# Softmax row sums in the attention of two layers: kept by ScalarE's exponentials and spread by one identity product, in place of products with ones

## The chip, the cores and the metric

The kernel runs on one core of one Trainium2 chip. The metric is the device time of the whole launch in microseconds. The engines are TensorE (PE, with its weight loads shown as PEld), VectorE (DVE), ScalarE (ACT), GpSimd (POOL) and SyncE (SP), whose DMA queue is SPq.

## The reference

Four layers, each an attention or a lookup ("xattn") and a feed-forward part, every one added to x through a gate. Layers 1 and 3 have the attention that the change touches; layer 1 has rotated queries and keys and a causal mask, layer 3 a given mask:

```python
# x: [32, 128, 128] (batch, position, width); H = 16 heads of width 8
q = split_heads(layernorm(x) @ Wq.T + bq)
k = split_heads(ctx @ Wk.T + bk)
v = split_heads(ctx @ Wv.T + bv)
# layer 1: q, k = rope(q), rope(k)
scores = jnp.einsum('bhqd,bhkd->bhqk', q, k) / sqrt(8)
scores = where(mask, scores, -inf)
probs = softmax(scores, axis=-1)
out = einsum('bhqk,bhkd->bhqd', probs, v).reshape(B, S, 128)
x = x + tanh(g_xattn[layer]) * (out @ Wo.T + bo)
```

## The kernel before

`build` runs nine stages one after the other, with a barrier between them; `stage_attn` (L949) is called for layer 1 (names `L1_...`) and for layer 3 (`L3_...`). The trace leaves the layer's number out, so both are `L_...`.

**Tiling.** The 32 batches are taken in 8 groups of 4 (`NG`, `GB`). The 16 heads of a batch are taken in 4 head groups of 4 heads (`NHG`). A step k is one batch and one head group: `hg = k % 4`, batch `b = k // 4`, 16 steps (`UG`) to a group of batches, 128 steps to a layer. All engines walk the same steps, each in its own order written out by hand, and wait for each other through counting semaphores.

**A step.** TensorE's `scores(k)` (L1328) makes a 128x512 tile of scores in one of two PSUM banks `sc`: 128 queries by 4 heads of 128 keys, and adds the mask by a second product. VectorE's `maximum(k)` (L1169) takes the negated row maxima of each head into `negm`. ScalarE's `exponent(k)` (L1255) does four exponentials of 128x128, one for each head, from `sc` into `E`. TensorE's `turn(k)` (L1337) transposes them into a bank `pt`, and ScalarE's `move(k)` (L1265) copies that to `PT`. TensorE's `attend(k)` (L1346) then adds to the bank `pp` of the batch: columns 0 to 127 get the products with the values `VZ`, columns 128 to 255 the products with ones `OZ`. Each is four products with 32 weight columns. The values and the ones stand at the places of their heads in otherwise zero tiles, so after four steps `pp` has all 16 heads, 8 rows each, and under 128 the row sum of the head, repeated in its 8 rows. VectorE's `invert(b)` (L1174) takes the reciprocal of the sums and `divide(b)` (L1178) multiplies.

**Order.** In TensorE's loop (L1364) step k brings `scores(k)`, `turn(k - 2)`, and in odd steps `attend(k - 5)` and `attend(k - 4)`; behind them stand, at the steps of `PUT`, the projections `put` of the next group, and at step 9 the output product `output` of the last one. `scores(k)` waits until the exponentials of step k - 2 are done, since there are two banks. ScalarE's loop (L1278) is `exponent(k)`, `move(k - 2)`, and at the steps of `UPPER` (3 and 7 in layer 1, 2 and 6 in layer 3) one more copy `upper` of keys or queries. VectorE's loop (L1211) has before `maximum(k)`: `invert` at every fourth step, `normalise` at step 0, `take` of the projections at the steps of `TAKE`, `add_output` at 11 and row statistics at 12; after it `divide` and the rest. GpSimd adds the two halves of the rotation (L1087, layer 1) and subtracts for the low parts of the split (L1089). SyncE writes the split keys and queries to memory and reads them back spread over partitions (`spread`, L1045); TensorE waits for them at the start of a group (L1365).

The attention of layer 2 (`stage_l2_attn`, L1677) has four exponentials of 128x128 with a kept sum (`accum_out`) at L1778.

Of the kernel before, what the change touches and what calls it, by code (L numbers as in the profile page):

```python
# [20 lines left out]
ACT = mybir.ActivationFunctionType  # L21
AX = mybir.AxisListType

B, S, D = 32, 128, 128
# [6 lines left out]
H, HD = 16, 8  # L31
# [913 lines left out]
NHG = 4  # L945
# [3 lines left out]
def stage_attn(nc, p, d, name, gate, rope, first):  # L949
# [4 lines left out]
    TAKE = {"k": 1, "kr": 2, "x": 3, "q": 5, "qr": 6, "v": 9}  # L954
    UPPER = {"k": 3, "q": 7} if rope else {"k": 2, "q": 6}
    OUT_PUT, OUT_TAKE = 9, 11
    TURN, ATTEND, DIVIDE = 2, 4, 8
    NU = NG * UG
    turn_of = {("const", 0): 0}
# [11 lines left out]
    with Stage(nc, name) as st:  # L971
# [8 lines left out]
        bias = {k: bias_all[:, i:i + 1] for i, k in enumerate(bn)}  # L980
        if rope:
# [8 lines left out]
        QS = [st.sb(f"QS{u}", [128, NHG, GD], F32R) for u in range(2)]  # L990
        VZ = [st.sb(f"VZ{u}", [128, GB, NHG * 128]) for u in range(2)]
        OZ = st.sb("OZ", [128, NHG * 128])
        negm = st.sb("negm", [128, 4, NHG])
        E = [st.sb(f"E{i}", [128, 512]) for i in range(4)]
        PT = [st.sb(f"PT{i}", [128, 512]) for i in range(4)]
# [6 lines left out]
        pp = [st.bank(f"pp{i}") for i in range(2)]  # L1002
        s = {k: st.sem(k) for k in (
            "w_in", "c_in0", "c_in1", "v_step", "xn_ready", "aux_full", "aux_free0", "aux_free1",
            "q_split", "k_split", "q_put", "k_put", "q_taken", "k_taken", "q_sum", "k_sum", "q_hi", "k_hi",
            "sc_ready", "max_ready", "exp_done", "pt_ready", "pt_moved", "av_done", "inv_done", "OT_ready", "v_ready", "const_ready", "zeroed", "VZ_zeroed", "QS_zeroed")}
        s_qin = [st.sem(f"q_in{u}") for u in range(2)]
        s_kin = [st.sem(f"k_in{u}") for u in range(2)]
        NW = 5 if rope else 4
# [66 lines left out]
        @block.gpsimd  # L1076
        def _(g):
            def zero(u):
                if first:
                    nc.gpsimd.memset(p.KS[u][:].bitcast(F32), 0.0).then_inc(s["zeroed"], 1)  # L1080
                else:
                    g.sem_inc(s["zeroed"], 1)

            def split(k, n):
                if rope:
                    g.wait_ge(s[k + "_taken"], n + 1)
                    nc.gpsimd.tensor_tensor(t1[k][:], t1[k][:], t2[k][:], ALU.add).then_inc(s[k + "_sum"], 1)  # L1087
                g.wait_ge(s[k + "_hi"], n + 1)
                nc.gpsimd.tensor_tensor(lo[k][:], t1[k][:], hi[k][:].bitcast(F32), ALU.subtract)\  # L1089
                    .then_inc(s[k + "_split"], 1)  # L1090

            def zero_rest(u):
                nc.gpsimd.memset(QS[u][3 * HW:128, :, :].bitcast(F32), 0.0).then_inc(s["QS_zeroed"], 1)

            zero(0)
            split("k", 0)
            split("q", 0)
            g.wait_ge(s["q_split"], 1)
            zero_rest(0)
            g.wait_ge(s["QS_zeroed"], 1)  # L1100
            zero(1)
            g.wait_ge(s["zeroed"], 2)
            zero_rest(1)
            g.wait_ge(s["QS_zeroed"], 2)
            credit(g, (tail.rstd_done, 2))
            for n in range(NG):
                if n + 1 < NG:
                    split("k", n + 1)
                if n + 1 < NG:
                    split("q", n + 1)  # L1110
                if n:
                    tail.gpsimd(g, n - 1, (n - 1) % 2)
            tail.gpsimd(g, NG - 1, (NG - 1) % 2)

        @block.vector
        def _(v):
# [52 lines left out]
            def maximum(k):  # L1169
                v.wait_ge(s["sc_ready"], k + 1)  # L1170
                nc.vector.tensor_reduce(negm[:, k % 4, :], sc[k % 2][:].rearrange("p (h k) -> p h k", h=NHG),  # L1171
                                        AX.X, ALU.max, negate=True).then_inc(s["max_ready"], 1)

            def invert(b):  # L1174
                v.wait_ge(s["av_done"], NHG * (b + 1))
                nc.vector.reciprocal(rinv[b % 2][:], pp[b % 2][:, 128:256]).then_inc(s["inv_done"], 1)

            def divide(b):  # L1178
# [32 lines left out]
            for n in range(NG):  # L1211
                for w in range(UG):
                    k = n * UG + w
                    b, due = (k - DIVIDE) // NHG, k >= DIVIDE and k % NHG == 0
                    if due:
                        invert(b)
                    if n + 1 < NG:
                        if w == 0:
                            normalise(n + 1)
                        for use in uses:  # L1220
                            if TAKE[use] == w:
                                take(use, n + 1)
                    if n:
                        if w == OUT_TAKE:
                            add_output(n - 1)
                        if w == OUT_TAKE + 1:
                            steps.need(mark)
                            mark = tail.row_stats(v, n - 1, (n - 1) % 2, steps)
                        if w == OUT_TAKE + 2:
                            steps.need(mark)  # L1230
                            tail.hand_over(v, n - 1, (n - 1) % 2)
                    maximum(k)
                    if due:
                        divide(b)
                    if n and w == OUT_TAKE:
                        mark = add_constant(n - 1)
                    if n and w == OUT_TAKE + 1:
                        steps.need(mark)
                        mark = tail.combine(v, n - 1, (n - 1) % 2, steps)
            for b in range(B - 2, B):  # L1240
                invert(b)
                divide(b)
# [5 lines left out]
        def _(a):  # L1248
# [4 lines left out]
                nc.scalar.activation(hi[k][:], t1[k][:], ACT.Copy).then_inc(s[k + "_hi"], 1)  # L1253

            def exponent(k):  # L1255
                e = E[k % 4]
                a.wait_ge(s["max_ready"], k + 1)
                if k >= 4:
                    a.wait_ge(s["pt_ready"], k - 3)
                for h in range(NHG):  # L1260
                    ins = nc.scalar.activation(e[:, h * 128:(h + 1) * 128], sc[k % 2][:, h * 128:(h + 1) * 128],  # L1261
                                               ACT.Exp, bias=negm[:, k % 4, h:h + 1])
                ins.then_inc(s["exp_done"], 1)

            def move(k):  # L1265
# [12 lines left out]
            for n in range(NG):  # L1278
                for w in range(UG):
                    k = n * UG + w  # L1280
# [10 lines left out]
        def _(t):  # L1291
# [54 lines left out]
            def attend(k):  # L1346
                n, j, hg = k // UG, k // NHG % GB, k % NHG
                if k % UG == 0:
                    t.wait_ge(s["v_ready"], n + 1)
                b = k // NHG  # L1350
                if hg == 0 and b >= 2:
                    t.wait_ge(s["OT_ready"], b - 1)
                t.wait_ge(s["pt_moved"], k + 1)
                for at, weights in ((0, VZ[n % 2][:, j, :]), (128, OZ[:])):
                    for c in range(NHG):
                        ins = nc.tensor.matmul(pp[b % 2][c * HW:(c + 1) * HW, at:at + 128],  # L1356
                                               weights[:, hg * 128 + c * HW:hg * 128 + (c + 1) * HW],
                                               PT[k % 4][:, c * 128:(c + 1) * 128], start=(hg == 0 and at == 0),
                                               stop=(hg == NHG - 1), skip_group_check=True)
                ins.then_inc(s["av_done"], 1)  # L1360

            for use in uses:
                put(use, 0)
            for n in range(NG):  # L1364
# [4 lines left out]
                for w in range(UG):  # L1369
                    k = n * UG + w  # L1370
# [1339 lines left out]
```

## Time and profile before

| | us |
|---|---|
| median of 3 runs | 2011.6 |
| lowest, highest | 2009.96, 2029.06 |
| profiled execution, its own time | 2011.66 |
| profiled execution, span of the trace | 2009.9 |
| TensorE busy in the span | 1648.7 (82%) |
| VectorE busy | 1288.4 (64%) |
| ScalarE busy | 1212.7 (60%) |
| GpSimd busy | 734.5 (37%) |

All times of the trace are microseconds from the start of the span. A busy time counts only instructions that compute. The two attention loops take about a quarter of the span; the other stages are not touched. A bracket at the end of a line of the timeline tells how long the engine sat idle before the instruction and which instruction ended the wait.

### The profile page before, as it was taken

The page shows a single profiled execution, that of the slowest core. Times are in us where ns is not written, and L with a number is a line of the kernel's source. Part 1 is how long each engine was busy: PE and PEld are TensorE (multiplying, and loading weights), DVE is VectorE, ACT ScalarE, POOL GpSimd, SP SyncE. Part 2 cuts the span into 40 slices and gives each one's busy share as a digit, 9 for nine tenths or more (in the row PEclk, how much of TensorE's full clock was granted, in tenths as well). Part 3 has the DMA queues.
Part 4 walks back from the last instruction along what each step waited for, and adds up shares of the span by engine and source line. Part 5 has one row for each costly group of instructions (what it writes and reads, how often), then busy time and mean ns, then how long its engine had stood idle before and what let it go on. Part 6 is the DMA issues. An engine that isn't in the chain of part 4 may idle for free. (4 is left out here: it accounts for less than half of the span.)

```text
span 2009.9 us, 38821 instructions
## 1 busy us (share of the span) xinstructions
PE 1648.7 (82%) x12780; PEld 1233.6 (61%) x12796; DVE 1288.4 (64%) x3301; ACT 1212.7 (60%) x4200; POOL 734.5 (37%) x671
## 2 busy tenths in 40 slices
PE   4399997699999399989599657998399998569993
PEld 4355554499999166666599655455266666447883
DVE  5599998488888666666477564123357766664444
ACT  2199996399999187878377522433178887223333
POOL 2155554255555411111278510012210100256774
PEclk9699999799999699999799776998599999569997
DMA  4310001100000333332000202000234331301114
GB/s 132 100 64 1 1 1 33 43 1 1 1 2 1 84 95 81 92 79 54 25 1 0 85 2 89 1 0 1 73 80 99 99 88 38 134 23 48 50 53 143
DMA packets 49360, 100.39 MB, mean 50 GB/s; under 512 B 8747, under 2 KB 16221, under 8 KB 47445
## 3 DMA queue, kind: packets, MB, share of 16 engines
q1 hardware_dynamic: 43126, 86.09, 15.4%
q0 software_dynamic: 4608, 9.32, 1.6%
q10 hardware_dynamic: 1440, 2.62, 0.6%
q8 instruction: 102, 1.67, 0.3%
q14 instruction: 84, 0.69, 0.1%
HBM read 69.19 MB, written 28.77 MB: 49 GB/s over the span
## 5 line engine op out<-in xcount | busy, mean ns | idle before, releaser
L592 ACT ACTIVATE B_E<-B_logits,B_m 128x32 f32<-128x32 f32 (+1 forms) x1792 | 362.6, 371 | 9.4 <-DVE B_m L561 8.3
L1261 ACT ACTIVATE L_E<-L_sc,L_negm 128x128 f32<-128x128 f32 x1024 | 299.0, 402 | 112.4 <-DVE L_negm L1171 111.7
L598 POOL TENSOR_TENSOR B_E<-B_E,B_r 128x512 f32<-128x512 f32 x256 | 267.6, 1046 | 259.2 <-DVE B_r L580 259.2
L1171 DVE TENSOR_REDUCE L_negm<-L_sc 128x4 f32<-128x512 f32 x256 | 174.4, 684 | 112.3 <-PE L_sc L1334 104.4
L561 DVE TENSOR_REDUCE B_m<-B_logits 128x16 f32<-128x512 f32 (+1 forms) x256 | 172.6, 675 | 37.8 <-PE B_logits L552 30.7
L1332 PE MATMUL L_sc<-KS,L_QS 128*128 128x512 f32 x256 | 141.6, 554 | 66.2 <-DMA L_QS<-L_qsplit 55.3
L575 DVE TENSOR_REDUCE B_r<-B_E 128x16 f32<-128x512 f32 (+1 forms) x256 | 172.7, 675 | 2.4 <-POOL B_E L598 1.3
L1269 ACT ACTIVATE L_PT<-L_pt 128x512 f32<-128x512 f32 x256 | 166.0, 651 | 0.6 <-PE L_pt L1342 0.6
L1342 PE MATMUL L_pt<-ident,L_E 128*128 128x128 f32 x1024 | 156.9, 276 | 1.6 <-ACT L_PT L1269 1.6
L550 PE MATMUL B_logits<-B_phihi,B_xhi 128*128 128x512 f32 x256 | 153.8, 601 | 5.2 <-DVE B_philo L537 2.5
L1342 PEld LDWEIGHTS L_pt<-ident,L_E 128*128 128x128 f32 x1024 | 123.8, 142 | 24.0 <-ACT L_E L1261 2.0
L920 PE MATMUL B_y<-Yt,B_CT 128*128 128x128 f32 x1024 | 135.4, 276 | 0.4 <-ACT B_CT L887 0.4
L680 PE MATMUL B_acc<-B_E,B_xn 128*128 128x512 f32 x256 | 131.1, 596 | 2.2 <-POOL B_E L598 1.3
L1618 ACT ACTIVATE F_part<-F_givenb,F_G 128x128 f32<-128x128 f32 x384 | 105.9, 389 | 36.6 <-PE F_givenb L1659 34.8
L920 PEld LDWEIGHTS B_y<-Yt,B_CT 128*128 128x128 f32 x1024 | 124.4, 192 | 0.9 <-DMA Yt<-slots_scratch 0.6
L1332 PEld LDWEIGHTS L_sc<-KS,L_QS 128*128 128x128 f32 x256 | 49.3, 193 | 105.6 <-DMA L_QS<-L_qsplit 59.2
L1536 POOL TENSOR_TENSOR F_given<-F_given,F_part 128x512 f32<-128x512 f32 x80 | 103.7, 1296 | 20.2 <-ACT F_part L1618 13.2
L1356 PE MATMUL L_pp<-L_PT,L_VZ 128*32 128x128 f32 x2048 | 106.3, 279 | 0.8 <-issue 0.8
L1356 PE MATMUL L_pp<-L_PT,L_OZ 128*32 128x128 f32 x2048 | 103.1, 273 | 0.0
L552 PE MATMUL B_logits<-B_philo,B_xhi 128*128 128x512 f32 x256 | 102.5, 400 | 0.0
L551 PE MATMUL B_logits<-B_phihi,B_xlo 128*128 128x512 f32 x256 | 102.3, 400 | 0.0
L1334 PE MATMUL L_sc<-L_mneg,ident 128*128 128x512 bf16 x256 | 102.0, 398 | 0.0
(350 smaller groups left out, 3709.9 us busy)
## 6 DMA issues: line engine op xcount, KB each, us to landing
KS<-L_ksplit SPq DMA_DIRECT2D x192, 64.0 KB
L_QS<-L_qsplit SPq DMA_DIRECT2D x42, 256.0 KB, 4.0
F_w<-in_F_w SPq DMA_DIRECT2D x4, 2048.0 KB, 9.0
ew<-in_expert_w SPq DMA_DIRECT2D x1, 4096.0 KB, 15.5
L_cT<-in_ctxT SPq DMA_DIRECT2D x16, 256.0 KB, 4.7
L_ksplit<-L_khi SPq DMA_DIRECT2D x16, 256.0 KB, 2.0
L_ksplit<-L_klo SPq DMA_DIRECT2D x16, 256.0 KB, 2.3
L_qsplit<-L_qhi SPq DMA_DIRECT2D x14, 256.0 KB, 2.7
```

What stands on the lines that cost most here:

```text
L550: nc.tensor.matmul(bank, xhi, self.hi[:, cols], start=True, stop=False)
L561: nc.vector.tensor_reduce(self.m[:, k % 4, :], lg, AX.X, ALU.max, negate=True).then_inc(self.max_done, 1)
L575: self.st.nc.vector.tensor_reduce(self.r[:, k % 2, :], self.grouped(k), AX.X, ALU.add).then_inc(self.sum_done, 1)
L592: ins = nc.scalar.activation(e[:, cols], self.bank(k)[:, cols], ACT.Exp, bias=self.m[:, k % 4, g:g + 1])
L598: self.st.nc.gpsimd.tensor_tensor(e, e, self.r[:, k % 2, :].unsqueeze(2) .to_broadcast([128, self.ng, self.size]), ALU.mult).then_inc(self ...
L920: ins = nc.tensor.matmul(y_ps[n % 2][:, j * 128:(j + 1) * 128], CT[k % 2][:, c * 128:(c + 1) * 128], Yt[:, 4 * q + c, :], start=(q == 0 an ...
L1171: nc.vector.tensor_reduce(negm[:, k % 4, :], sc[k % 2][:].rearrange("p (h k) -> p h k", h=NHG), AX.X, ALU.max, negate=True).then_inc(s["ma ...
L1261: ins = nc.scalar.activation(e[:, h * 128:(h + 1) * 128], sc[k % 2][:, h * 128:(h + 1) * 128], ACT.Exp, bias=negm[:, k % 4, h:h + 1])
L1269: nc.scalar.activation(PT[k % 4][:], pt[k % 2][:], ACT.Copy).then_inc(s["pt_moved"], 1)
L1332: nc.tensor.matmul(sc[k % 2][:], QS[n % 2][:, hg, j * 128:(j + 1) * 128], p.KS[n % 2][:, hg, :, j * 128:(j + 1) * 128], start=True, stop=F ...
L1342: ins = nc.tensor.transpose(pt[k % 2][:, c * 128:(c + 1) * 128], E[k % 4][:, c * 128:(c + 1) * 128], p.ident[:])
L1356: ins = nc.tensor.matmul(pp[b % 2][c * HW:(c + 1) * HW, at:at + 128], weights[:, hg * 128 + c * HW:hg * 128 + (c + 1) * HW], PT[k % 4][:, ...
```

## The change

In both layers `attend` leaves out the products with ones for every head group (`COUNTED` holds all four). The exponentials keep their row sums instead (`accum_out`), one number per row and head, in `su[b % 2][:, head, head group]`, 128x16. When the last step of a batch has its exponentials, `widen(b)` on VectorE copies the 16 numbers of each row into `sub`, 128x128, each repeated 8 times. After `attend` of the batch's last head group TensorE multiplies `sub` as weights by the identity: it is transposed into columns 128 to 255 of `pp`, where the ones products put the sums before. `widen(b)` stands on VectorE behind `maximum(4b + 6)`; the identity product stands on TensorE in step 4b + 7. `invert` waits for it. ScalarE waits before the first exponentials of a batch for `widen` of the batch two before. Two small tiles are cleared once by GpSimd.

```diff
+    COUNTED = (0, 1, 2, 3)
...
+        su = [st.sb(f"su{u}", [128, NHG, NHG]) for u in range(2)]
+        sub = [st.sb(f"sub{u}", [128, NHG, NHG, HD]) for u in range(2)]
...
             zero(0)
+            for u in range(2):
+                nc.gpsimd.memset(su[u][:], 0.0).then_inc(s["su_zeroed"], 1)
             split("k", 0)
...
+            def widen(b):
+                v.wait_ge(s["exp_done"], NHG * b + max(COUNTED) + 1)
+                if b >= 2:
+                    v.wait_ge(s["sum_done"], b - 1)
+                nc.vector.tensor_copy(sub[b % 2][:], su[b % 2][:].unsqueeze(3).to_broadcast([128, NHG, NHG, HD]))\
+                    .then_inc(s["sums_wide"], 1)
+
             def invert(b):
-                v.wait_ge(s["av_done"], NHG * (b + 1))
+                v.wait_ge(s["sum_done"], b + 1)
...
                     if due:
                         divide(b)
+                    if k >= 6 and k % NHG == 2:
+                        widen((k - 6) // NHG)
...
+            widen(B - 1)
             for b in range(B - 2, B):
...
             def exponent(k):
-                e = E[k % 4]
+                e, b, hg = E[k % 4], k // NHG, k % NHG
                 a.wait_ge(s["max_ready"], k + 1)
+                if k == 0:
+                    a.wait_ge(s["su_zeroed"], 2)
+                if hg == 0 and b >= 2:
+                    a.wait_ge(s["sums_wide"], b - 1)
...
                     ins = nc.scalar.activation(e[:, h * 128:(h + 1) * 128], sc[k % 2][:, h * 128:(h + 1) * 128],
-                                               ACT.Exp, bias=negm[:, k % 4, h:h + 1])
+                                               ACT.Exp, bias=negm[:, k % 4, h:h + 1],
+                                               accum_out=su[b % 2][:, h, hg:hg + 1] if hg in COUNTED else None)
...
-                for at, weights in ((0, VZ[n % 2][:, j, :]), (128, OZ[:])):
+                for at, weights in ((0, VZ[n % 2][:, j, :]), (128, OZ[:]))[:1 if hg in COUNTED else 2]:
...
                 ins.then_inc(s["av_done"], 1)
+                if hg == NHG - 1:
+                    t.wait_ge(s["sums_wide"], b + 1)
+                    nc.tensor.matmul(pp[b % 2][:, 128:256], sub[b % 2][:].rearrange("p c g d -> p (c g d)"), p.ident[:],
+                                     start=False, stop=True, skip_group_check=True).then_inc(s["sum_done"], 1)
```

## Rows read from the trace of the kernel before

**Rows 1.** Busy us per engine, then clock, DMA share, GB/s, in both loops.
```profile
698.00:960.00 262.00, 241.34 (x2974) 165.53 (x2976) 171.08 (x361) 207.74 (x654) 42.85 (x35) 0.98 0.33 77
1461.00:1703.00 242.00, 228.62 (x2943) 160.07 (x2945) 163.00 (x347) 209.03 (x654) 24.89 (x21) 0.99 0.34 83
```

**Rows 2.** Page, costliest groups: count, busy us, mean ns, idle before and releaser.
```profile
L1261 ACT ACTIVATE L_E<-L_sc,L_negm 128x128 f32<-128x128 f32 x1024 | 299.0, 402 | 112.4 <-DVE L_negm L1171 111.7
```

**Rows 3.** Timeline, second loop, end of a group: start us, length, what.
```profile
1516.73 0.50 PE L1332 MATMUL L_sc<-KS,L_QS 128*128 128x512 f32 x1 [0.31 <-ACT L_E L1261]
...
1516.98 1.21 ACT L1261 ACTIVATE L_E<-L_sc,L_negm 128x128 f32<-128x128 f32 x4
...
1517.87 0.43 PE L1356 MATMUL L_pp<-L_PT,L_VZ 128*32 128x128 f32 x8
1517.98 0.70 ACT L1269 ACTIVATE L_PT<-L_pt 128x512 f32<-128x512 f32 x1
1518.11 0.40 PE L1356 MATMUL L_pp<-L_PT,L_OZ 128*32 128x128 f32 x8
1518.33 0.40 PE L1356 MATMUL L_pp<-L_PT,L_VZ 128*32 128x128 f32 x8
1518.46 1.25 ACT L1261 ACTIVATE L_E<-L_sc,L_negm 128x128 f32<-128x128 f32 x4
...
1519.02 0.96 DVE L1176 RECIPROCAL L_rinv<-L_pp 128x128 f32<-128x128 f32 x1 [0.82 <-PE L_pp L1356]
...
1519.89 1.02 DVE L1123 TENSOR_SCALAR L_xn<-X,mean,rstd 128x128 f32<-128x128 f32 x4
1520.91 0.49 PE L1332 MATMUL L_sc<-KS,L_QS 128*128 128x512 f32 x1 [1.96 <-DMA L_QS<-L_qsplit]
...
1522.39 1.14 ACT L1261 ACTIVATE L_E<-L_sc,L_negm 128x128 f32<-128x128 f32 x4 [2.20 <-DVE L_negm L1171]
```

**Rows 4.** Timeline of ScalarE in layer 2's attention, exponentials with a kept sum.
```profile
1160.70 0.37 ACT L1778 ACTIVATE A_E<-A_sc,A_negm 128x128 f32<-128x128 f32 x1 [3.37 <-DVE A_negm L1737]
...
1161.06 0.36 ACT L1778 ACTIVATE A_E<-A_sc,A_negm 128x128 f32<-128x128 f32 x1
...
1161.74 0.37 ACT L1778 ACTIVATE A_E<-A_sc,A_negm 128x128 f32<-128x128 f32 x1
1161.99 0.21 ACT L1778 ACTIVATION_READ_ACCUMULATOR A_E<-A_sc,A_negm 128x1 f32 x1
```

**Rows 5.** Timeline, second loop: the output product of a group.
```profile
1507.60 1.16 PE L1324 MATMUL L_aux<-L_W,L_OT 128*128 128x128 f32 x8
```

**Rows 6.** Line 1130: a broadcast copy; ns min/median/max, first and last start.
```profile
L1130 DVE COPY L_bvb<-L_bias x2: 216/218/221, 668.1 to 1435.5; 128x128 f32<-128x128 f32 x2
```

**Rows 7.** Timeline, first loop, from step 1 to step 2 of a group.
```profile
832.09 1.14 ACT L1261 ACTIVATE L_E<-L_sc,L_negm 128x128 f32<-128x128 f32 x4 [0.33 <-DVE L_negm L1171]
...
832.51 1.12 PE L1315 MATMUL L_aux<-L_cT,L_W 128*128 128x512 f32 x2
...
834.56 1.27 POOL L1087 TENSOR_TENSOR L_t1k<-L_t1k,L_t2k 128x512 f32<-128x512 f32 x1 [10.37 <-DVEq L1167]
...
835.29 1.14 ACT L1261 ACTIVATE L_E<-L_sc,L_negm 128x128 f32<-128x128 f32 x4 [1.58 <-DVE L_negm L1171]
```

**Rows 8.** Timeline: first exponentials of groups 1 and 7, both loops.
```profile
730.10 1.14 ACT L1261 ACTIVATE L_E<-L_sc,L_negm 128x128 f32<-128x128 f32 x4 [3.09 <-DVE L_negm L1171]
...
930.61 1.14 ACT L1261 ACTIVATE L_E<-L_sc,L_negm 128x128 f32<-128x128 f32 x4 [2.85 <-DVE L_negm L1171]
...
1490.88 1.14 ACT L1261 ACTIVATE L_E<-L_sc,L_negm 128x128 f32<-128x128 f32 x4 [1.34 <-DVE L_negm L1171]
...
1674.64 1.14 ACT L1261 ACTIVATE L_E<-L_sc,L_negm 128x128 f32<-128x128 f32 x4 [0.35 <-DVE L_negm L1171]
```

**Rows 9.** TensorE alone, two stretches: us, busy, clock, DMA share, GB/s.
```profile
792.15:795.56 3.41, 1.18 (x7) 0.99 0.62 145
795.56:798.98 3.42, 3.42 (x12) 0.51 0.00 0
```

More of the change, by code:

```diff
@@ L1005, in stage_attn @@
             "q_split", "k_split", "q_put", "k_put", "q_taken", "k_taken", "q_sum", "k_sum", "q_hi", "k_hi",
-            "sc_ready", "max_ready", "exp_done", "pt_ready", "pt_moved", "av_done", "inv_done", "OT_ready", "v_ready", "const_ready", "zeroed", "VZ_zeroed", "QS_zeroed")}
+            "sc_ready", "max_ready", "exp_done", "pt_ready", "pt_moved", "av_done", "inv_done", "OT_ready", "v_ready", "const_ready", "zeroed", "VZ_zeroed", "QS_zeroed", "su_zeroed", "sums_wide", "sum_done")}
         s_qin = [st.sem(f"q_in{u}") for u in range(2)]
```

## The prediction

> **What bounds the kernel now.** I read the busy times of the two attention loops first, because only they are touched. The first runs from 698 to 960 us, the second from 1461 to 1703 us [rows 1]. The reader is to see two nearly full engines: TensorE is busy 241.3 of 262 us and 228.6 of 242, at a granted clock of 0.98 and 0.99, and ScalarE 207.7 and 209.0. ScalarE's idle time is thus only 54.3 + 33.0 = 87.3 us, in both loops together. Next come the page's costliest groups, which say whom ScalarE waits for: the row maxima of VectorE [rows 2]. Last I read a stretch of the second loop in order of time, around the end of a group [rows 3]. There a step k costs ScalarE the distance from one exponential group to the next, 1518.46 - 1516.98 = 1.48 us, with no gap: four exponentials, then from 1517.98 the copy of a transposed tile. So in such stretches ScalarE sets the pace already. TensorE sets it where projections, the output product or the loads of the next group get in between. From the first exponential of group 1 to that of group 7 the loops take (930.61 - 730.10)/6 = 33.42 us a group and (1674.64 - 1490.88)/6 = 30.63 us [rows 8], where 16 x 1.48 would be 23.7. The difference is where TensorE's saving could count.
>
> **What is removed.** Per step the ones products: eight short records that take TensorE from 1518.11 to 1518.33, 0.22 us [rows 3], so 256 x 0.22 = 56 us. They stand right in front of the next projection or the next scores.
>
> **What is added on TensorE.** One product of a 128x128 fp32 tile with the identity per batch, 64 in all. The nearest row is the output product of the same size, four of which are eight records in 1.16 us [rows 5]. A record alone lasts about 0.28 us (the ones' eight, which run four abreast, 0.40 together), so they follow at (1.16 - 0.28)/7 = 0.126 us and a product of two costs 0.25, 16 us in all: net 40 us less on TensorE. From below one pitch, 0.126 us (8 us in all); from above the whole two records without overlap, 0.56 (36 us). I take 0.25, since other products stand on both sides of it.
>
> **What is added on VectorE.** One copy of 128x128 with a broadcast input per batch; the same form took 0.22 us [rows 6], 14 us in all. It stands behind the maximum of step 4b+6, one step before the identity product wants it, and its own wait (exponentials of step 4b+4) is over before that maximum can start. Behind it in the queue are the maxima of the next steps. VectorE has 334 busy of 504 us [rows 1], so I cost it at nothing; without that cover it costs at most its 14 us. The reciprocal now waits for the identity product instead of the last ones product: it starts about 0.44 us earlier (two products fewer in front) less 0.25, so no later. The two small clears of the sums on GpSimd stand once per layer ahead of the key split; bounds 0 and 0.5 us each, I take 0.
>
> **What is added on ScalarE.** This is the term that decides. Layer 2's attention in this kernel has the same exponentials (128x128 from PSUM with a bias per row) with a kept sum. Each is followed by an accumulator read of 0.21 us; the fourth starts 1161.74 - 1160.70 = 1.04 us after the first, 0.347 us each, and the fourth read ends at 1162.20, 1.50 us after the start [rows 4]. Without the sum four take 1.14 us [rows 7]; with 0.37 for the last, the length of one in rows 4, (1.14 - 0.37)/3 = 0.257 each. The read costs 0.09 us, a step 0.36, and 256 steps 92 us. Lower bound: zero, if the reads hid in ScalarE's gaps to the last one; upper bound: the whole read, 4 x 0.21 x 256 = 215 us, which the rows 4 themselves exclude. I take 0.36: a step becomes 1.84 us for ScalarE.
> The Trainium skill, ScalarE: Activation LUTs, What ACT_TABLE_LOAD costs, prices an ACTIVATE with a pointer bias at 280 ns + 0.833 ns an element, overlapping its neighbour by 93 ns: 294 ns for 128 elements, where the rows show 257. It names the accumulator output but gives no price for it. By that page alone ScalarE would lose nothing; the rows say 92 us.
>
> **The sum.** 92 us of new work do not fit into 87.3 us of idle time, even if every gap were filled: 416.8 + 92 = 509 against 504, a floor of +5. Not every gap can be filled. I follow a group of the second loop by ScalarE's order, with 1.84 us a step: 16 x 1.84 = 29.5; the two extra copies that split keys and queries 0.5 each, 1.0; step 1 stays 0.35 late behind the key projection; the output product at step 9 and the statistics at step 12 leave about 0.2 each, since a chain through TensorE is longer than three of ScalarE's steps: exponentials done 1.50 us after their start, 1.14 of scores and transposes (1516.73 to 1517.87), 0.48 of value products, 1.16 of output product [rows 5], 1.48 from scores to exponentials (1520.91 to 1522.39) [rows 3], 5.8 against 3 x 1.84 = 5.5. At the group's end the reciprocal and the next normalisation precede the first maximum: 1519.02 to 1520.91 and 0.7 for the maximum, 2.6 us [rows 3]. The reciprocal can start 1.50 + 1.14 + 0.48 + 0.25 and some 0.25 of hand-overs, 3.6 us, after step 13's exponentials: 6.2 against 5.5, 0.7 late. Together 29.5 + 1.0 + 0.35 + 0.4 + 0.7 = 32.0 us against 30.6. Over six groups (the last of them has no normalisation) this gives +8. The first group takes 1461 to 1490.88 now, 29 us with less of TensorE's work in it, against 16 x 1.84 + 1.0 + 0.7 and about 0.8 at the first projection, 32: +3. The last has 15 x 1.84 = 27.6 and 0.4 against 1674.64 to 1703 less 3 of drain, 25.4 [rows 1, 8]: +3. Second loop: +14.
> In the first loop TensorE's saving counts. Between steps 1 and 2 the second key projection waits for the two ones products, and with it the take on VectorE, the maximum and ScalarE; that projection starts at 832.51, and the exponentials go from 832.09 to 835.29, 3.20 us, 1.58 of them idle [rows 7]. That becomes 3.20 - 0.44 = 2.76, above 1.84; the same at step 6 about 2.1. The sum becomes 29.5 + 1.0 + 0.1 at step 1 + 0.9 at step 2 + 0.25 at step 6 + 0.4 + 0.7 = 32.8 us a group. But groups end when the next queries land: before, the first scores wait for that DMA [rows 3, 8], and it is issued as the splits are, which ScalarE does 0.25 us later. So 33.4 becomes 33.7: six groups +1.5, first +1, last +2. First loop: +4.5. The drain after the last exponentials has four ones products less and one identity product, 0.6 us shorter in each loop: -1. Sum: 14 + 4.5 - 1 = +17.5.
> To this I add +3 for the clock. Around 794 us TensorE was busy 1.18 of 3.41 us while it waited for queries, and in the next 3.42 us the granted clock was 0.51, that is the 1.2 GHz level instead of 2.4 [rows 9]. Each such fall costs about half of 3.4 us, 1.7. A TensorE that works 0.8 instead of 0.95 of the time has emptier group ends; two more such falls in 14 group ends are my guess. The profiled execution took 2011.66 us with a span of 2009.9, and the median of the runs is 2011.6, so both stand alike: 2011.6 + 20.5 = **2032 us**.
>
> **The rivals.** (a) The gaps are filled almost wholly. What speaks for it: nearly all idle time of ScalarE is put down to the maxima, which come earlier when TensorE has 40 us less. Against: the chain at the group's end. It gives +5 to +10, 2017 to 2022. (b) The reads of the accumulator cost nothing here, because the engine hides them behind the copy. Then ScalarE's 1.48 us stays, TensorE's net 40 us comes off wherever it leads, and the time goes down to 1972 at best; between +20 at 0.09 us a read and some -35 at none it passes -20 at a read of about 0.025 us, and from there down it decides. Against it stand all 32 pairs of rows like those of [rows 4]. (c) The clock falls at most group ends: 12 more x 1.7 = +20, 2053. For it: the one fall shown followed a wait of this kind. Against: most of the 14 waits in the loops have none, as the clocks 0.98 and 0.99 show. (d) The broadcast copy is held up. At step 2 of the first loop GpSimd's sum of the rotated keys starts at 834.56 and runs 1.27 us [rows 7], just where the copy will stand; if the copy waits for its end it loses some 0.6 us, at steps 2 and 6, of which slack takes most: +3 to +6, 2036.
> The Trainium skill, SBUF — State Buffer, Who interferes with whom, says a copy with source and destination in SBUF may take the port pair that VectorE shares with GpSimd, and that the second to issue waits for the whole instruction. By that rule (d) would be certain in the first loop; no row of before shows it for this copy.
>
> **How the numbers follow.** Chances: the forecast with its own range 2022 to 2043, 0.52; (a) 0.22; (b) 0.04; (c) 0.10; (d) 0.12. The range goes from just under (a)'s floor, 2014, to nearly (c), 2052, and leaves out (b) and part of (c). About 1%, 20 us, is what a measurement of this kernel can tell from no change: below 2031.7 lie (a), nearly half of the forecast's own range, a little of (d), 0.43; faster by over 1% is only (b), 0.04; slower 0.53.
>
> **What would show it.** Right: 1024 accumulator reads in the loops' exponential line, exponential groups 1.50 us long and 1.84 us apart where nothing else waits; ScalarE busy about 250 us a loop; TensorE's busy time down by 20 us a loop; no idle time before the identity product put down to the broadcast copy; the second loop longer by 14, the first by 4. Wrong: a pitch of 1.48 kept; TensorE's clock below 0.95 in a loop; idle time of ScalarE above 30 us in the second loop, which would mean a chain that I cost too low.

## The result, and the profile after

| | before | after |
|---|---|---|
| median of nine runs each, us | 2015.8 (2000.7 to 2029.1) | 2040.5 (2037.0 to 2042.7) |
| span of the profiled execution, us | 2009.9 | 2037.8 |

After to before is 1.0122, with a 95% interval of 1.0093 to 1.0152: slower by about 1.2%, 24.7 us.

Both loops by engine in the trace after, with the columns of [rows 1] (ScalarE's busy time is the fourth pair, the clock stands behind GpSimd's):

```profile
706.33:972.50 266.17, 229.47 (x2050) 145.67 (x2048) 182.40 (x393) 251.28 (x1166) 42.77 (x35) 0.99 0.31 75
1473.75:1733.20 259.45, 221.86 (x2022) 141.18 (x2020) 167.41 (x379) 250.49 (x1166) 24.85 (x21) 0.99 0.32 77
```

ScalarE went from 207.7 and 209.0 us to 251.3 and 250.5; in the second loop it is idle for only 9 us of 259. TensorE's clock is as good as before. The costliest groups of the page after, which answer to [rows 2]:

```profile
L1280 ACT ACTIVATE L_E<-L_sc,L_negm 128x128 f32<-128x128 f32 x1024 | 392.2, 490 | 47.1 <-DVE L_negm L1176 47.1
L1280 ACT ACTIVATION_READ_ACCUMULATOR L_E<-L_sc,L_negm 128x1 f32 x1024 | 306.9, 330 | 0.0
```

The wait for the maxima fell from 111.7 [rows 2] to 47.1 us, which is where 64.6 us of ScalarE's new work found cover; the rest, about 20 us, made the loops longer. The end of a group of the second loop, which answers to [rows 3]:

```profile
1534.55 0.64 PE L1376 MATMUL L_pp<-L_PT,L_VZ 128*32 128x128 f32 x16
...
1535.12 0.49 PE L1383 MATMUL L_pp<-ident,L_sub 128*128 128x128 f32 x2
...
1535.39 0.47 PE L1352 MATMUL L_sc<-KS,L_QS 128*128 128x512 f32 x1
1535.53 0.46 ACT L1280 ACTIVATE L_E<-L_sc,L_negm 128x128 f32<-128x128 f32 x1
1535.65 0.96 DVE L1188 RECIPROCAL L_rinv<-L_pp 128x128 f32<-128x128 f32 x1 [0.78 <-PE L_pp L1383]
...
1536.52 1.02 DVE L1128 TENSOR_SCALAR L_xn<-X,mean,rstd 128x128 f32<-128x128 f32 x4
...
1537.46 0.68 DVE L1176 TENSOR_REDUCE L_negm<-L_sc 128x4 f32<-128x512 f32 x1
...
1538.18 0.37 ACT L1280 ACTIVATE L_E<-L_sc,L_negm 128x128 f32<-128x128 f32 x1 [0.56 <-DVE L_negm L1176]
...
1538.54 0.36 ACT L1280 ACTIVATE L_E<-L_sc,L_negm 128x128 f32<-128x128 f32 x1
...
1539.56 0.61 ACT L1289 ACTIVATE L_PT<-L_pt 128x512 f32<-128x512 f32 x1
...
1540.04 0.39 ACT L1280 ACTIVATE L_E<-L_sc,L_negm 128x128 f32<-128x128 f32 x1
```

Read it from the bottom. Two exponentials are 1538.54 - 1538.18 = 0.36 us apart, and two groups of four 1540.04 - 1538.18 = 1.86: the new pitch of a step. The one real gap is at the group's end, 1538.18 - 1535.53 = 2.65, of which 0.56 idle. The chain ahead of it: value products, identity product, reciprocal, normalisation, maximum. The cost of the identity product on TensorE is the distance from its start at 1535.12 to the next scores' weight load, which starts at 1535.36, 0.24 us later.

All loop times below go from the first group of exponentials to the last of a layer, read from ScalarE's timeline in the same way for each kernel. Where the profiled 27.9 us went:

| stretch, us | before | after | |
|---|---|---|---|
| start to first loop | 698.2 | 706.3 | +8.1 |
| first loop (layer 1) | 258.6 | 261.6 | +3.0 |
| between the loops | 505.2 | 505.8 | +0.6 |
| second loop (layer 3) | 237.9 | 254.8 | +16.9 |
| last exponentials to the end | 309.9 | 309.3 | -0.7 |

The first line lies ahead of the changed code, in one burst of TensorE in an earlier stage: 160 products into the tile `M_y`. Here is TensorE there, before and then after, counting only what touches this tile (busy us of TensorE, of its weight loads and of ScalarE, then clock, DMA share, GB/s):

```profile
368.30:381.10 12.80, 12.60 (x160) 7.43 (x160) 1.85 (x4) 0.98 0.01 1
```

```profile
369.10:390.30 21.20, 20.98 (x160) 11.17 (x160) 1.89 (x4) 0.50 0.00 1
```

The same products take 12.6 us at a granted clock of 0.98 and 21.0 us at 0.50, the 1.2 GHz level instead of 2.4: these 8.4 us make up the first line, but for 0.3. Whether the change brings them is open. The second pair of executions, below, has the low level on both sides (706.0 us before, 705.1 after, as the first line counts). But all nine profiled executions of `after` and of kernels made from it have it there, and only one of the four of `before` and of kernels made from it. The two loops' +19.9 lie in the changed code.

### The profile page after: what moved, and what is told of

Its sections match the earlier page's. It is cut to its first block and busy times, and to the rows that moved or that the text cites. A ratio compares the mean times of both kernels' runs of the same rounds, so it can differ in the third digit from the quotient of the medians.

```text
span 2037.8 us, 36151 instructions
## 1 busy us (share of the span) xinstructions
PE 1640.9 (81%) x10876; PEld 1198.4 (59%) x10876; DVE 1307.8 (64%) x3365; ACT 1299.3 (64%) x5224; POOL 734.4 (36%) x675
## 5 line engine op out<-in xcount | busy, mean ns | idle before, releaser
L1280 ACT ACTIVATE L_E<-L_sc,L_negm 128x128 f32<-128x128 f32 x1024 | 392.2, 490 | 47.1 <-DVE L_negm L1176 47.1
L1280 ACT ACTIVATION_READ_ACCUMULATOR L_E<-L_sc,L_negm 128x1 f32 x1024 | 306.9, 330 | 0.0
L1352 PE MATMUL L_sc<-KS,L_QS 128*128 128x512 f32 x256 | 134.2, 524 | 103.8 <-ACT L_E L1280 60.5
L1289 ACT ACTIVATE L_PT<-L_pt 128x512 f32<-128x512 f32 x256 | 188.0, 736 | 0.6 <-PE L_pt L1362 0.6
L1362 PEld LDWEIGHTS L_pt<-ident,L_E 128*128 128x128 f32 x1024 | 113.4, 141 | 28.5 <-ACT L_E L1280 2.9
L1683 PE MATMUL F_givenb<-F_WrT,F_xnT 128*128 128x128 f32 x768 | 98.7, 284 | 3.0 <-issue 1.6
## 6 DMA issues: line engine op xcount, KB each, us to landing
L_QS<-L_qsplit SPq DMA_DIRECT2D x42, 256.0 KB, 3.9
L_cT<-in_ctxT SPq DMA_DIRECT2D x16, 256.0 KB, 4.6
L_ksplit<-L_khi SPq DMA_DIRECT2D x16, 256.0 KB, 2.0
L_ksplit<-L_klo SPq DMA_DIRECT2D x16, 256.0 KB, 2.3
L_qsplit<-L_qhi SPq DMA_DIRECT2D x14, 256.0 KB, 2.7
```

What stands on the lines that cost most here:

```text
L1289: nc.scalar.activation(PT[k % 4][:], pt[k % 2][:], ACT.Copy).then_inc(s["pt_moved"], 1)
L1352: nc.tensor.matmul(sc[k % 2][:], QS[n % 2][:, hg, j * 128:(j + 1) * 128], p.KS[n % 2][:, hg, :, j * 128:(j + 1) * 128], start=True, stop=F ...
L1362: ins = nc.tensor.transpose(pt[k % 2][:, c * 128:(c + 1) * 128], E[k % 4][:, c * 128:(c + 1) * 128], p.ident[:])
```

## The experiments

The base of each is named with its edit. Kernels of one set ran on the same chip, and sets differ: in the second set the kernel before has loops of 247.3 and 233.6 us instead of 258.6 and 237.9. So loops are compared within a set where there is a partner; the first set has none. A loop time is that of one profiled execution. Steadier is the quiet group of the second loop, one whose start waits for no late queries: `before` has 29.92 us in both of its profiles, `after` 32.32 and 32.27. A ratio is one of whole-kernel times to the kernel before, run beside it.

**First set: take away the reads, add the reads, take away the spread, count half of the head groups.** After, without the kept sums (the tiles `su` are filled with ones, so the normalisation is left out of the computation):

```diff
-                                               ACT.Exp, bias=negm[:, k % 4, h:h + 1],
-                                               accum_out=su[b % 2][:, h, hg:hg + 1] if hg in COUNTED else None)
+                                               ACT.Exp, bias=negm[:, k % 4, h:h + 1])
```

> The changed kernel with exponentials that keep no sum; the tile of sums holds ones, so the output is not the softmax. Everything else of the change stays (no ones products, broadcast copy, identity product). Theory (the accumulator reads cost 0.09 us each and decide): exponential groups 1.48 us apart instead of 1.85, groups of the second loop about 29.2 us, of the first about 32.6, the whole kernel 13 to 20 us under the kernel before, ratio 0.990 to 0.994. Rival (the new chain through broadcast copy, identity product and reciprocal costs the time): ratio stays above 1.008. Rival (TensorE's saving is worth nothing): ratio 1.000.

Measured 1.0035 (0.9997 to 1.0073) where 0.990 to 0.994 was expected; by the ratio alone the second rival, a saving worth nothing, fits. The second loop went as expected, 233.1 us with quiet groups of 29.15. The first did not: 268.3 us with groups of 35.2 where 32.6 was expected, 5.0 to 6.8 us from the last step of a group to the first of the next, and a granted clock of 0.94.

Before, with the kept sums written to `su` and nothing reading them:

```diff
-                                               ACT.Exp, bias=negm[:, k % 4, h:h + 1])
+                                               ACT.Exp, bias=negm[:, k % 4, h:h + 1],
+                                               accum_out=su[b % 2][:, h, hg:hg + 1])
```

> The kernel before, with its ones products, and the exponentials keep their sums in a tile that nobody reads. Theory: ScalarE has the 92 us of reads without TensorE's saving: slower than the changed kernel by about 11 us, ratio to the kernel before 1.013 to 1.019, the second loop's groups near 32.8 us, the first loop's near 34.4, with 3.2 us kept between steps 1 and 2. Rival (the copy and identity product carry the loss): ratio under 1.005.

Measured 1.0129 (1.0072 to 1.0186), second loop 255.8, quiet groups of 32.59, first loop 265.5. The reads alone thus give a loss as large as the result above, and in the second loop the whole of it. The exchange of products, which this kernel doesn't have, took only some 1 us more off that loop in `after`, 254.8 in another set. A miss: between steps 1 and 2 of the first loop 3.2 us should have stayed, and it was anything from 2.13 to 3.59; where it was 2.13, the group had started without waiting for queries.

After, without the broadcast copy and the identity product, `invert` reading the value columns (the output is not normalised by the sums):

```diff
-                v.wait_ge(s["sum_done"], b + 1)
-                nc.vector.reciprocal(rinv[b % 2][:], pp[b % 2][:, 128:256]).then_inc(s["inv_done"], 1)
+                v.wait_ge(s["av_done"], NHG * (b + 1))
+                nc.vector.reciprocal(rinv[b % 2][:], pp[b % 2][:, 0:128]).then_inc(s["inv_done"], 1)
...
-                    nc.tensor.matmul(pp[b % 2][:, 128:256], sub[b % 2][:].rearrange("p c g d -> p (c g d)"), p.ident[:],
-                                     start=False, stop=True, skip_group_check=True).then_inc(s["sum_done"], 1)
```

> The changed kernel without the broadcast copy and the identity product; the reciprocal waits for the value products and takes them as its input, so the output is not the softmax. Theory: these two cost only the 0.25 us of TensorE in the chains at a group's end and at steps 8 and 12: about 0.4 us a group, 6 us under the changed kernel, ratio to the kernel before 1.007 to 1.011. Rival (they carry the loss): ratio at or below 1.000.

Measured 1.0115 (1.0048 to 1.0181), at the upper edge of what was expected. Groups of the second loop 31.7 instead of 32.3: 0.6 us a group from the chain ahead of the reciprocal, slightly more than expected. Step 1 to step 2 of the first loop is 2.77 in the median without the copy and 2.71 in `after` with it, so the copy costs nothing there.

After, with `COUNTED = (0, 1)`, so that the sums of head groups 2 and 3 come from ones products again:

```diff
-    COUNTED = (0, 1, 2, 3)
+    COUNTED = (0, 1)
```

> The changed kernel with sums kept for head groups 0 and 1 only, ones products for 2 and 3; computes the same. Theory: half of the reads (46 us of ScalarE), half of the ones products saved, the identity product in full: second loop's groups about 31.0 us, first loop's 33.2, ratio to the kernel before 0.998 to 1.005. Rival (a loss that comes with the identity product and not with the reads): ratio 1.010, as with all four.

Measured 1.0203 (1.0146 to 1.026), the slowest of all, second loop 261.9. My expectation had added up each engine's work and not the chain. The timeline of this kernel, second loop, from step 11 to step 12 of a group:

```profile
1600.00 0.42 PE L1376 MATMUL L_pp<-L_PT,L_VZ 128*32 128x128 f32 x8
...
1600.67 0.40 PE L1376 MATMUL L_pp<-L_PT,L_OZ 128*32 128x128 f32 x8
...
1601.01 0.49 PE L1383 MATMUL L_pp<-ident,L_sub 128*128 128x128 f32 x2
...
1601.53 0.96 DVE L1188 RECIPROCAL L_rinv<-L_pp 128x128 f32<-128x128 f32 x1 [0.62 <-PE L_pp L1383]
...
1603.13 0.67 DVE L1176 TENSOR_REDUCE L_negm<-L_sc 128x4 f32<-128x512 f32 x1
...
1603.84 0.37 ACT L1280 ACTIVATE L_E<-L_sc,L_negm 128x128 f32<-128x128 f32 x1 [1.51 <-DVE L_negm L1176]
```

From the first value product to the reciprocal it is 1.53 us; `after` has 1535.65 - 1534.55 = 1.10 and before 1519.02 - 1517.87 = 1.15 [rows 3]. Head groups 2 and 3 are the pair that `attend` does last in a batch, so both the ones products and the identity product now stand ahead of the reciprocal; the next maximum is behind the reciprocal, and ScalarE is idle for 1.51 us. The reads that this kernel saves, at steps 14 and 15 of a group, bring nothing either: the chain runs on, and the quiet group's end is 3.46 us instead of 2.65. Three of the seven group ends of this profile's second loop took 4.5 to 4.9 us; in all three the granted clock was 0.50, the 1.2 GHz level, while the last products of the group ran (from 1539 to 1541 us in one of them), so part of the 261.9 us is the clock, 0.98 over this loop.

**Second set: before and after again, the first edit again, and the other half counted.** One execution of each. The first two are unchanged kernels, as partners:

> The kernel before, unchanged, as a control on the chip of this set: how long its two loops last here. Theory (the loops themselves are steady from chip to chip, the spread between chips lies in the other stages and in the first loop's DMA waits): second loop 238 to 239 us from first to last exponentials, first loop 259 to 270.

> The changed kernel, unchanged, as a control on the same chip. Theory: second loop 255 to 256 us, 17 more than the kernel before; first loop 260 to 264, at most 4 more than the kernel before and less where DMA waits are long.

Measured 2027.7 and 2063.0 us. Loops 247.3 and 233.6 before, 255.8 and 253.8 after: +8.5 and +20.2. All four loops came out shorter than expected, and both differences larger: the loops are not steady from set to set, the first least of all.

> Once more the changed kernel whose exponentials keep no sum (sums of ones, so the output is not the softmax), next to controls on the same chip. Theory (without the reads the first loop ends its groups waiting for the queries' DMA, since the splits go out no earlier): second loop 233 to 234 us, first loop within 3 us of the kernel before on this chip, with waits of 3 us and more at the group ends. Rival (the first loop's 35 us a group came from that chip): first loop under 256 us.

Measured 2031.6 us, second loop 231.6, first 252.7. The first loop is 5.4 us above before's where at most 3 was expected, and below the rival's 256: the 35 us a group of the first set were not the kernel's alone. In the second loop the exchange of products gives 233.6 - 231.6 = 2.0 us and the reads cost 253.8 - 231.6 = 22.2 us. A quiet group is 29.15 us as in the first set, 0.77 less than before's; the last groups give most of that back waiting for queries. In the first loop the reads cost only 255.8 - 252.7 = 3.1 us. What became of the saving is visible at the group's end of this kernel, second loop and then first:

```profile
1524.15 1.14 ACT L1280 ACTIVATE L_E<-L_sc,L_negm 128x128 f32<-128x128 f32 x4 [1.29 <-DVE L_negm L1176]
```

```profile
890.88 1.27 SPq L1028 DMA_DIRECT2D L_QS<-L_qsplit  x3
...
891.57 0.96 DVE L1188 RECIPROCAL L_rinv<-L_pp 128x128 f32<-128x128 f32 x1 [0.78 <-PE L_pp L1382]
...
892.44 1.02 DVE L1128 TENSOR_SCALAR L_xn<-X,mean,rstd 128x128 f32<-128x128 f32 x4
896.13 0.79 PE L1351 MATMUL L_sc<-KS,L_QS 128*128 128x512 f32 x1 [4.60 <-DMA L_QS<-L_qsplit]
...
898.14 1.14 ACT L1280 ACTIVATE L_E<-L_sc,L_negm 128x128 f32<-128x128 f32 x4 [5.35 <-DVE L_negm L1176]
```

In the second loop the chain through reciprocal, normalisation and maximum ends the group in 3.04 us, as it does before (3.09). In the first, the last part of the queries is issued from 890.88 on and the scores wait for it until 896.13: all that TensorE gained ahead of it is waited away. That is the longest of the seven group ends, 7.09 us from step 15 to step 0; together they take 30.4 us against 21.3 before, while the seven stretches from step 5 to 6 give back 6.2. The first loop is 5.4 us longer than before's. Part of that is the clock of this loop, 0.96 (columns as in [rows 1]):

```profile
706.00:964.00 258.00, 230.83 (x2050) 149.21 (x2048) 181.94 (x394) 207.60 (x654) 42.76 (x35) 0.96 0.31 78
```

After, with the pair counted that is done last:

```diff
-    COUNTED = (0, 1, 2, 3)
+    COUNTED = (2, 3)
```

> The changed kernel with sums kept for head groups 2 and 3 only, ones products for 0 and 1; computes the same. As many reads and ones products as with 0 and 1, but the ones products are saved in front of the reciprocal (steps 3, 7, 11, 15 on TensorE) and kept where there is slack. Theory (a chain of scores, products, sum, reciprocal, maximum sets the pace at every fourth step): second loop near 246 us against 262 with head groups 0 and 1. Rival (only the number of reads and products counts): 262 as with 0 and 1.

Measured 2052.3 us, loops 253.2 and 244.4. The same number of reads and of ones products as with (0, 1), and the second loop is 261.9 - 244.4 = 17.5 us shorter. The two ran on different chips, so compare quiet groups too: 32.93 against 30.98 us, which makes some 15 of the 17.5; the rest goes with the low clock at three group ends of the (0, 1) kernel. The place of the ones products decides, as that timeline says. The 246 us expected were close.

**Third set: the reciprocal behind the maximum.** If the reciprocal ahead of the maximum sets the group's end, then moving it should give time. Three bases: before, after, and after without the reads (not normalised, as above).

```diff
                     if due:
-                        invert(b)
...
                     maximum(k)
                     if due:
+                        invert(b)
                         divide(b)
```

> The kernel before, with its ones products, and on VectorE the reciprocal of a batch stands behind the maximum of its step instead of in front; computes the same. Theory (the reciprocal's 0.96 us in front of the maximum is what the end of a group and step 12 wait for): step 12 about 1.9 us instead of 2.55, the group end about 2.2 instead of 3.1, groups of the second loop 28 to 29 us instead of 29.9, both loops together 15 to 22 us less, ratio to the kernel before 0.989 to 0.993. Rival (TensorE's own time sets the pace): ratio 1.000.

> The changed kernel with the reciprocal behind the maximum; computes the same. Theory: ScalarE's steps stay 1.85 us and the stalls at step 12 (2.35) and at the group end (2.65) go: second loop's groups 31.0 us instead of 32.3, the loop 245 us. It stays slower than the kernel before with the same edit by some 15 us in the second loop.

> The changed kernel without kept sums (sums of ones, so the output is not the softmax) and with the reciprocal behind the maximum. It tells what TensorE's saved products are worth once the reciprocal is out of the chain. Theory: 0.2 us less of TensorE at the projection steps and nothing elsewhere, since ScalarE's 1.48 us stays: second loop 1 to 4 us under the kernel before with the same edit. Rival (the reciprocal had eaten the saving): 8 us and more under it.

Measured 1.0028 (1.0002 to 1.0055) on before, and in one execution each 2044.5 us on after and 2025.1 without the reads; the kernel before took 2019.1 beside them. Second loops: 242.6, 256.0 and 240.5. The first two are misses: no gain on before, and on after 256.0 where 245 was expected, though it stays 13.4 above before with the same edit, near the 15 expected. The third is a hit: 2.1 us under before with the same edit, where 1 to 4 was expected and the rival wanted 8. So this chip too puts TensorE's saving in the second loop at 2 us, and the reads at 256.0 - 240.5 = 15.5. The expected waits did go, on before: the group's end fell from 3.09 to 1.87, step 12 from 2.55 to 1.93. But groups of the second loop became longer, 31.1 instead of 29.9; on after they stayed at 32.3. The timeline of before with this edit, second loop, steps 8 to 9:

```profile
1540.32 0.69 DVE L1171 TENSOR_REDUCE L_negm<-L_sc 128x4 f32<-128x512 f32 x1 [2.35 <-PE L_sc L1333]
...
1540.93 0.95 DVE L1176 RECIPROCAL L_rinv<-L_pp 128x128 f32<-128x128 f32 x1
...
1541.98 0.29 DVE L1183 TENSOR_TENSOR L_OT<-L_pp,L_rinv 128x128 f32<-128x128 f32 x1
...
1542.19 0.87 DVE L1146 COPY L_VZ<-L_aux 128x128 f32<-128x128 f32 x4
...
1543.30 0.69 DVE L1171 TENSOR_REDUCE L_negm<-L_sc 128x4 f32<-128x512 f32 x1 [0.24 <-DVE L_VZ L1146]
...
1544.03 0.62 ACT L1260 ACTIVATE L_E<-L_sc,L_negm 128x128 f32<-128x128 f32 x2 [1.35 <-DVE L_negm L1171]
```

Between two maxima VectorE now does the reciprocal, the division and the copy of the values, and the maxima are 2.98 us apart; in the unmoved kernel of the second set:

```profile
1532.62 0.69 DVE L1171 TENSOR_REDUCE L_negm<-L_sc 128x4 f32<-128x512 f32 x1 [0.56 <-PE L_sc L1334]
...
1534.54 0.69 DVE L1171 TENSOR_REDUCE L_negm<-L_sc 128x4 f32<-128x512 f32 x1 [0.24 <-DVE L_VZ L1146]
```

1.92 us. Steps 8 to 9 got 1.06 us longer, steps 0 to 1 and 12 to 13 a further 1.0 each, and those 3.0 are more than the 1.2 + 0.6 gained (step 4 to 5 got 0.55 longer and step 9 to 10 0.50 shorter). The reciprocal before the maximum stands in time in which VectorE waits for the scores anyway: even with it in front, 0.56 us of that wait are left ahead of the maximum at 1532.62. My expectation had counted where it leaves and not where it lands.

## Why the prediction was right, step by step

The time was predicted at 2032, within 2022 to 2043, and came out at 2040.5. The decisive reason holds: the reads do not fit into ScalarE's idle time, whatever TensorE saves. Around it the sizes agree less well, and some luck is in the total. The forecast added 20.5 us to 2011.6; the medians of nine differ by 24.7, from 2015.8. Of the +20.5 the loops and their drains were to be 17.5 and the clock 3. In the profiles the loops are +19.9 in one pair and +28.7 in the other, and the clock took nothing there, but 8.1 us of the first pair lie in a stage that the sum did not treat.

- **The read costs 0.09 us, a step 0.36.** Right: where nothing else waits, steps are about 1.85 us apart in every kernel with reads and 1.48 in every one without. The reads' own records sum to 307 us, but they overlap the next exponential; ScalarE gained 43.5 and 41.5 us a loop, 85 in all, by its union of busy time. Rival (b) is out.
- **The floor, 92 us against 87.3 of idle time, and not all gaps can be filled.** Right, and isolated: in the second loop the reads cost 22.2 us of their 46 (`after` against the same kernel without reads, one chip; 15.5 on another with the reciprocal moved), the others filled gaps. In the first loop they cost 3.1 and 1.9 us in the same two comparisons.
- **Second loop, predicted 32.0 a group and +14.** Measured 32.3 a group and +16.9, +20.2 on the second chip. By terms: step 1 is not late (1.85, predicted 0.35 late); step 10 is 0.30 late and step 12 0.50, where 0.2 each was set down; the end 0.80 where 0.7 was. With 16 x 1.85, two copies of 0.52 and 0.05 at step 9 that is 32.3. The mis-sized term is step 12, which was costed as the chain of the output product, with 0.2 left. The row statistics stand there between the reciprocal and the maximum:

```profile
1559.46 0.49 PE L1383 MATMUL L_pp<-ident,L_sub 128*128 128x128 f32 x2
...
1559.98 0.96 DVE L1188 RECIPROCAL L_rinv<-L_pp 128x128 f32<-128x128 f32 x1
...
1560.86 0.81 DVE L184 BATCH_NORM_STATS2 L_bn<-X 128x6 f32<-128x128 f32 x4
...
1561.58 0.67 DVE L1176 TENSOR_REDUCE L_negm<-L_sc 128x4 f32<-128x512 f32 x1
...
1562.29 0.37 ACT L1280 ACTIVATE L_E<-L_sc,L_negm 128x128 f32<-128x128 f32 x1 [0.34 <-DVE L_negm L1176]
```

  From identity product to exponentials that is 2.83 us by VectorE's order, a chain of the same kind as at the group's end (1538.18 - 1535.12 = 3.06). Taking the identity product and the copy away shortened step 12 from 2.35 to 2.18 and the group's end from 2.65 to 2.26. At the end the chain itself was well sized: reciprocal 1535.65 - 1531.83 = 3.82 us after the start of step 13's exponentials (predicted 3.6), and step 15 to step 0 is 2.65. What did not come is the earlier reciprocal. By the prediction two products fewer, less the identity product, are worth 0.44 - 0.25 = 0.19 us; from the first value product to the reciprocal it is 1.10 us after and 1.15 before, so 0.05.
- **First loop, predicted +4.5.** Measured +3.0 in the first pair and +8.5 in the second, so the agreement of the first is partly luck. Step 1 to 2 came down to 2.71 in the median of the first profile, where 2.76 was predicted, but to 1.99 in that of the second; step 6 needed nothing (1.86, predicted 2.1). Both kernels vary. Before has 258.6 or 247.3, mostly by when the queries land: from the last step of a group to the first of the next it took 3.1 to 4.8 us in the first profile and 2.1 to 3.6 in the second. `after` has 261.6 and 255.8; of these 5.8 us 1.9 lie at the group ends and 3.3 between steps 1 and 2. That the group's end was bound by that DMA was right for the profile that the sum was made from, and too good a cover for other executions.
- **The drain, -1.** Not borne out: from the last exponentials of a loop to the last output product it is 6.65 us after and 6.68 before, in both loops of the first pair. The four ones products are gone, but the last exponentials have their reads; without reads it is 6.30.
- **The clock, +3.** Not borne out: 0.99 in both loops after. Falls of the kind of [rows 9] were seen elsewhere, in the first loop of the kernels without reads, which had the longest waits for queries: 0.94, 0.96 and 0.97 over that loop in the three sets, against 0.98 and 0.99 before (with sums counted for head groups 0 and 1 it was 0.96 too). So the falls came mostly without the reads, not at the slower pace that I argued from; what decides on them is not shown. The sum came near partly because this term stood in for the undersized step 12.
- **TensorE, 20 us of busy time a loop less.** About half of it: in the first pair 11.9 and 6.8 us; 9.7 and 8.9 on one chip (windows of equal content). The products themselves are as counted, 0.24 us for an identity product. The groups of TensorE in the second loop, before and then after, second set (count, busy us and mean ns, then idle time before them):

```profile
L1332 PE MATMUL L_sc<-KS,L_QS 128*128 128x512 f32 x127 | 67.6, 533 | 7.3 <-ACT L_E L1261 5.1 <-DMA L_QS<-L_qsplit 1.7
L1356 PE MATMUL L_pp<-L_PT,L_VZ 128*32 128x128 f32 x1024 | 52.9, 279 | 0.0
L1356 PE MATMUL L_pp<-L_PT,L_OZ 128*32 128x128 f32 x1024 | 51.4, 273 | 0.0
```

```profile
L1352 PE MATMUL L_sc<-KS,L_QS 128*128 128x512 f32 x127 | 64.1, 505 | 35.3 <-ACT L_E L1280 33.2 <-DMA L_QS<-L_qsplit 1.0
L1376 PE MATMUL L_pp<-L_PT,L_VZ 128*32 128x128 f32 x1024 | 41.1, 279 | 0.0
L1383 PE MATMUL L_pp<-ident,L_sub 128*128 128x128 f32 x64 | 15.6, 326 | 0.0
```

  What TensorE saved it spends waiting, 33.2 us for ScalarE's exponentials instead of 5.1. That records that stand alone count their whole length as busy, and those in a row overlap, would explain why the busy time fell by less than counted; it was not measured by itself.
- **The broadcast copy.** Rival (d)'s mechanism is there and costs nothing. First loop, step 1 to step 2:

```profile
809.32 0.37 ACT L1280 ACTIVATE L_E<-L_sc,L_negm 128x128 f32<-128x128 f32 x1
...
811.35 1.27 POOL L1090 TENSOR_TENSOR L_t1k<-L_t1k,L_t2k 128x512 f32<-128x512 f32 x1 [10.85 <-DVEq L1172]
...
811.97 0.74 DVE L1183 COPY L_sub<-L_su 128x128 f32<-128x128 f32 x1
812.09 0.37 ACT L1280 ACTIVATE L_E<-L_sc,L_negm 128x128 f32<-128x128 f32 x1 [0.77 <-DVE L_negm L1176]
```

  The copy takes 0.74 us beside GpSimd's sum and 0.22 where GpSimd is idle: it ends 0.09 us after GpSimd's instruction. Thirteen of the 64 copies meet such a sum, all in the first loop, and each ends 0.08 to 0.09 us behind it. The Trainium skill, SBUF — State Buffer, Who interferes with whom, has such a copy wait for the whole instruction of GpSimd; the trace agrees, and shows beside it that the next maximum had slack enough.

What stays open: why the queries land later in the first loop in one set than in another, and with it how the first loop's loss divides between reads and products; whether the low clock in the burst ahead of the loops comes with the change; and what makes the stretch behind the second loop differ (309 to 310 us in the first pair and the third set, 332 to 338 in the others). A comparison of second loops within a set rests on none of these.

## What to carry to other kernels

Price a new instruction by the pitch of a group that has it against one that has not, not by its own record, and set it against the idle time of its engine: where that idle time is smaller, the change loses whatever the other engine saves. An engine that is 92 to 94% busy can still not be the bound; here 20 us of its work in the second loop, as counted beforehand, were worth 2 us. The group's end hung there on a chain over VectorE or on a DMA; that this is the reason is read from the timelines, since no run took the whole chain away. When a piece of a chain is removed, put back or moved, ask what stands directly ahead of the next instruction of the pacing engine: the same work in another place was worth some 15 us.

## What the runs showed of the hardware

The accumulator read's record, 0.33 us in the mean, is no cost: the pitch of exponentials rises by 0.09 us. The records grow by themselves in a row without a wait: in the second loop of `after` an exponential goes from 0.37 us at 1505.86 to 0.66 at 1521.70, while the exponentials of a step stay 0.343 us apart, and is back at 0.37 behind the next wait. So the mean of 490 ns in the group row is a length and not a price.

One burst of 160 products of TensorE took 12.6 us at a granted clock of 0.98 and 21.0 us at 0.50, in executions of otherwise equal stages: a single stretch at the lower level is worth as much as a third of the change measured here.
